# Softmax denominators: summed over key tiles on VectorE and GpSimd, one ones-matmul group per unit

## The reference

```
x = x + attn_a(layernorm(x));  x = x + ffn(layernorm(x))
x = x + attn_b(layernorm(x));  x = x + ffn(layernorm(x))
attn: qkv = h @ Wqkv + b; 16 heads of 32; scores = q k^T / sqrt(32), causal; softmax; @ v; @ Wo + bo
ffn:  (silu(h @ Wg^T) * (h @ Wu^T)) @ Wd^T, hidden 2048
```

## Time and profile before

| | |
|---|---|
| device time, median of 2 runs | 2245.22 us (2243.66 to 2246.78) |
| profiled execution | span 2243.9 us; its own device time is not recorded apart from the two above |
| TensorE busy | 2137.2 us (95%) |
| TensorE weight loads | 1502.9 us (67%) |
| VectorE busy | 1269.9 us (57%) |
| ScalarE busy | 531.7 us (24%) |
| GpSimd busy | 668.7 us (30%) |
| DMA | 135.10 MB in packets, mean 60 GB/s |
| granted TensorE clock | 0.982 in the mean |

### The profile page before, as it was taken

The page is one execution under the profiler, slowest core; times in us unless marked ns, Lnnn a source line. Parts: engine busy times, 40 slices in busy tenths (PEclk is TensorE's granted clock), DMA queues, the critical chain, the costliest instruction groups (busy, mean ns, idle before and its releaser), DMA issues.

```text
span 2243.9 us, 34194 instructions
## 1 busy us (share of the span) xinstructions
PE 2137.2 (95%) x11056; PEld 1502.9 (67%) x11056; DVE 1269.9 (57%) x2475; ACT 531.7 (24%) x1076; POOL 668.7 (30%) x508
## 2 busy tenths in 40 slices
PE   6999989999999999999989999999999999999998
PEld 5555478888755447888765554788886554578886
DVE  6767464545576646445447665544555666454444
ACT  1344410000144441000104454100011444310001
POOL 3323223332312322323231233232323223233332
PEclk9999999999999989999999999999999999999998
DMA  4332101111323211111142321111113232011112
GB/s 129 89 86 67 30 29 57 48 57 38 77 68 77 67 39 38 48 48 47 66 124 68 77 67 39 38 52 43 47 39 77 68 89 63 29 47 47 57 38 94
DMA packets 59745, 135.10 MB, mean 60 GB/s; under 512 B 10784, under 2 KB 11808, under 8 KB 59552
## 3 DMA queue, kind: packets, MB, share of 16 engines
q1 hardware_dynamic: 59552, 132.71, 20.9%
HBM read 77.62 MB, written 4.19 MB: 36 GB/s over the span
## 4 chain that ended last, share of the span: by engine, by line
PE 84%; issue 7%; DVE 4%; POOL 2%; ACT 1%; DMA 1%; SPq 1%; DVEq 0%; POOLq 0%; ACTq 0%
PE ring L872 13%; PE ring L873 13%; PE ring L874 13%; PE bank L982 12%; PE ring L936 8%; PE bank L960 7%; PE bank L872 6%; PE bank L873 6%; PE bank L874 6%; PE ring L863 1%; DVE attn L645 1%; POOL area L426 1%; DVE xn L682 1%; ACT prob L543 1%; DVE xn L645 1%
## 5 line engine op out<-in xcount | busy, mean ns | idle before, releaser
L872 PE MATMUL ring<-xt_hi,area 128*128 128x512 f32 x1248 | 492.0, 394 | 11.2 <-DVE xt_lo L654 8.1
L873 PE MATMUL ring<-xt_lo,area 128*128 128x512 f32 x1248 | 488.3, 391 | 0.0
L874 PE MATMUL ring<-xt_hi,area 128*128 128x512 f32 x1248 | 488.1, 391 | 0.0
L682 DVE CUSTOM_DVE_ANT_0 xn<-ring,mask_row 128x128 bf16<-128x128 f32 (+7 forms) x512 | 374.9, 750 | 131.4 <-PE ring L936 126.6
L543 ACT ACTIVATE prob<-bank 128x512 f32<-128x512 f32 (+3 forms) x768 | 335.4, 489 | 345.0 <-PE bank L960 344.0
L424 POOL TENSOR_SCALAR area<-w_stage 128x1024 fp32r<-128x1024 f32 x131 | 145.5, 1111 | 820.2 <-PE bank L874 432.5
L743 DVE TENSOR_TENSOR prob<-prob,ring 128x512 f32<-128x512 f32 x128 | 88.0, 687 | 450.2 <-ACT prob L561 450.1
L426 POOL TENSOR_TENSOR area<-w_stage,area 128x1024 fp32r<-128x1024 f32 x131 | 322.6, 2462 | 10.9
L561 ACT ACTIVATE prob<-ring 128x512 f32<-128x512 f32 x128 | 76.6, 598 | 999.5 <-PE ring L874 999.5
L872 PEld LDWEIGHTS ring<-xt_hi,area 128*128 128x128 f32 x1248 | 235.5, 189 | 71.3 <-issue 9.8
L874 PEld LDWEIGHTS ring<-xt_hi,area 128*128 128x128 f32 x1248 | 235.4, 189 | 49.8
(11 more groups left out here) (76 smaller groups left out, 2088.0 us busy)
## 6 DMA issues: line engine op xcount, KB each, us to landing
w_stage<-ffn_w SPq DMA_DIRECT2D x96, 512.0 KB, 3.3
area<-kq_parts SPq DMA_DIRECT2D x336, 128.0 KB, 2.3
w_stage<-attn_w SPq DMA_DIRECT2D x35, 512.0 KB, 3.3
x<-x_in SPq DMA_DIRECT2D x24, 256.0 KB, 3.7
area<-attn SPq DMA_DIRECT2D x48, 128.0 KB, 2.3
out<-x SPq DMA_DIRECT2D x16, 256.0 KB, 2.1
bias_rows<-row_bias SPq DMA_DIRECT2D x10, 256.0 KB, 4.1
area<-nm_hi SPq DMA_DIRECT2D x32, 8.0 KB, 1.8
```

The costliest lines, as they stand in the source:

```text
L682: dve.tensor_tensor_reduce(out=sum_out[:, RING[name] % 2, 0:keys], in0=src[:, 0:keys], in1=mask_row[:, TOKENS - keys:], scale=1.0, scalar= ...
L872: pe.matmul(dst, ah, bh, start=first and k == 0, stop=False)
L873: pe.matmul(dst, ah, bl, start=False, stop=False)
L874: ins = pe.matmul(dst, al, bh, start=False, stop=last and k == n - 1)
```

## The change

- TensorE no longer multiplies each step's `prob` with ones. VectorE (heads 0 and 1, `add_low`) and GpSimd (heads 2 and 3, `add_high`) add the `prob` tiles of a unit's key steps into `prob_sum` in SBUF, and one group of 4 ones-matmuls per unit (`denominators`) sums that over the partitions.
- `prob` gets a third buffer; the exponentials of a step wait for the values and for both sums of the step three back.
- `evacuate` copies out_bank only. ScalarE makes a first reciprocal as exp(-ln(den)) (`first_recip`), from one activation table set that is preloaded, and VectorE refines it with one Newton step folded into the normalisation: attn*r, then -den*r, then (that + 2)*attn*r.
- GpSimd's queue is written anew: masks, sums, weight split and attn splits interleaved by key step. VectorE's too. The attn of unit 6 is now split by VectorE, and the points of the last unit move by two half steps.

The core of it, with 12 columns of indentation taken off:

```diff
 def points(u):
...
-        return [9, 11, 13, 15, 23, 27]
+        return [11, 13, 15, 17, 25, 27]
...
-RECIPS = 8
+SPLIT_AFTER = (3, 1)
+ATTN_AFTER = {(5, 2): 0, (5, 3): 1, (5, 4): 2, (5, 5): 3, (6, 3): 4, (7, 2): 5}
+NORMALISE_AT = 3
+EXP_TABLE = "natural_log_exp_and_others"
...
-RECIPS_FROM = 6
-RECIPS_BETWEEN = 6
...
+PROB_BUFS = 3
+HALF = GH // 2
+ADD_BASE = [sum(key_tiles(v) - 1 for v in range(u)) for u in range(UNITS + 1)]
+ADDS = ADD_BASE[UNITS]
+POOL_SPLITS = UNITS - CHUNKS
+def added_through(u, j):
...
-        prob = sb("prob", [P, 2, GH, CHUNK])
+        prob = sb("prob", [P, PROB_BUFS, GH, CHUNK])
+        prob_sum = sb("prob_sum", [P, GH, CHUNK])
...
-    tile = prob[:, step % 2, :, d * P:(d + 1) * P]
+    tile = prob[:, step % PROB_BUFS, :, d * P:(d + 1) * P]
...
+def add_high(it, u, j):
+    step = J_BASE[u] + j
+    d = j - CT * unit(u)[1]
+    off = max(0, d) * P
+    heads = slice(HALF, GH)
+    wait_alone(pool, prob_ready, it * S2_STEPS + GH * (step + 1))
+    if d >= 0:
+        wait_alone(pool, mask_done, it * UNITS * CT + u * CT + d + 1)
+    new = prob[:, step % PROB_BUFS, heads, off:]
+    if j > 1:
+        wait_alone(pool, added_high, it * ADDS + ADD_BASE[u] + j - 1)
+        pool.tensor_tensor(prob_sum[:, heads, off:], prob_sum[:, heads, off:], new, ALU.add
+                           ).then_inc(added_high, 1)
+        return
+    old = prob[:, (step - 1) % PROB_BUFS, heads, :]
+    if u:
+        wait_alone(pool, sums_done, it * UNITS + u)
+    if off:
+        pool.tensor_copy(prob_sum[:, heads, :off], old[:, :, :off])
+    pool.tensor_tensor(prob_sum[:, heads, off:], old[:, :, off:], new, ALU.add).then_inc(added_high, 1)
 def split_attn(it, u):
...
-        if u in SPLIT_BEFORE:
-            split_weights(it, SPLIT_BEFORE[u])
-        for w in {5: range(5), 7: range(5, 7)}.get(u, ()):
-            split_attn(it, w)
-        for d in range(CT):
-            mask_probs(it, u, d)
-            if u == UNITS - 1 and d == 1:
+        for j in range(key_tiles(u)):
+            if j >= CT * unit(u)[1]:
+                mask_probs(it, u, j - CT * unit(u)[1])
+            if j:
+                add_high(it, u, j)
+            if j == SPLIT_AFTER[unit(u)[1]] and u in SPLIT_BEFORE:
+                split_weights(it, SPLIT_BEFORE[u])
+            if (u, j) in ATTN_AFTER:
+                split_attn(it, ATTN_AFTER[u, j])
+            if u == UNITS - 1 and j == CT + 1:
...
     def exps(u, j, heads):
...
-        if step >= 2:
-            act.wait_ge(pv_done, it * KEY_STEPS + step - 1)
+        if step >= PROB_BUFS:
+            added = it * ADDS + added_through(*step_of(step - PROB_BUFS))
+            act.wait_ge(pv_done, it * KEY_STEPS + step - PROB_BUFS + 1)
+            act.wait_ge(added_low, added)
+            act.wait_ge(added_high, added)
...
-            act.activation(prob[:, step % 2, h, off:], bank[n % 2][:, off:], ACT.Exp,
+            act.activation(prob[:, step % PROB_BUFS, h, off:], bank[n % 2][:, off:], ACT.Exp,
...
     def evacuate(u):
...
+        act.activation(attn[:, g, c * CHUNK:(c + 1) * CHUNK], out_bank[:, :], ACT.Copy
+                       ).then_inc(evacuated, 1)
+    def first_recip(u):
+        act.wait_ge(sums_done, it * UNITS + u + 1)
...
-        act.activation(recip[:, :], den_bank[:, :], ACT.Copy)
-        act.activation(attn[:, g, c * CHUNK:(c + 1) * CHUNK], out_bank[:, :], ACT.Copy
-                       ).then_inc(evacuated, 1)
+        act.activation(recip[:, :], den_bank[:, :], ACT.Ln).then_inc(log_done, 1)
+        act.wait_ge(log_done, it * UNITS + u + 1)
+        act.activation(recip[:, :], recip[:, :], ACT.Exp, scale=-1.0).then_inc(recip_done, 1)
     def silus(s, t):
...
+            if u and j == 1:
+                first_recip(u - 1)
...
+    evacuate(UNITS - 1)
+    first_recip(UNITS - 1)
...
-    evacuate(UNITS - 1)
...
-    load_table(ACT.Exp)
+    act.preload_act_table_set(EXP_TABLE)
...
-    def recip_part(u, n):
-        if n == 0:
-            dve.wait_ge(evacuated, it * UNITS + u + 1)
-        cols = slice(n * CHUNK // RECIPS, (n + 1) * CHUNK // RECIPS)
-        dve.reciprocal(recip[:, cols], recip[:, cols]).then_inc(recip_done, 1)
+    def add_low(u, j):
+        step = J_BASE[u] + j
+        d = j - CT * unit(u)[1]
+        off = max(0, d) * P
+        heads = slice(0, HALF)
+        dve.wait_ge(prob_ready, it * S2_STEPS + GH * step + HALF)
+        if d >= 0:
+            dve.wait_ge(mask_done, it * UNITS * CT + u * CT + d + 1)
+        new = prob[:, step % PROB_BUFS, heads, off:]
+        if j > 1:
+            dve.wait_ge(added_low, it * ADDS + ADD_BASE[u] + j - 1)
+            dve.tensor_tensor(prob_sum[:, heads, off:], prob_sum[:, heads, off:], new, ALU.add
+                              ).then_inc(added_low, 1)
+            return
+        old = prob[:, (step - 1) % PROB_BUFS, heads, :]
+        if u:
+            dve.wait_ge(sums_done, it * UNITS + u)
+        if off:
+            dve.tensor_copy(prob_sum[:, heads, :off], old[:, :, :off])
+        dve.tensor_tensor(prob_sum[:, heads, off:], old[:, :, off:], new, ALU.add).then_inc(added_low, 1)
     def normalise_attn(u):
...
-        dve.wait_ge(recip_done, (it * UNITS + u + 1) * RECIPS)
-        dve.tensor_tensor(attn[:, g, cols], attn[:, g, cols], recip[:, :], ALU.mult).then_inc(attn_ready, 1)
-    def split_last():
-        g, c = unit(UNITS - 1)
+        n = it * UNITS + u + 1
+        dve.wait_ge(recip_done, n)
+        dve.wait_ge(evacuated, n)
+        dve.tensor_tensor(attn[:, g, cols], attn[:, g, cols], recip[:, :], ALU.mult).then_inc(scaled, 1)
+        dve.wait_ge(scaled, n)
+        dve.scalar_tensor_tensor(recip[:, :], den_bank[:, :], -1.0, recip[:, :], ALU.mult, ALU.mult
+                                 ).then_inc(newton_done, 1)
+        dve.wait_ge(newton_done, n)
+        dve.scalar_tensor_tensor(attn[:, g, cols], recip[:, :], 2.0, attn[:, g, cols], ALU.add, ALU.mult
+                                 ).then_inc(attn_ready, 1)
+    def split_last(u):
+        g, c = unit(u)
...
-        dve.wait_ge(attn_ready, it * UNITS + UNITS)
+        dve.wait_ge(side_full, side_done(it, ("k", UNITS - 1)))
+        dve.wait_ge(attn_ready, it * UNITS + u + 1)
...
-        dve.wait_ge(last_hi_done, it + 1)
+        dve.wait_ge(last_hi_done, it * CHUNKS + c + 1)
...
-    for u in range(-1, UNITS - 1):
-        parts = list(range(RECIPS)) if u > 0 else []
-        def some_recips(count):
-            for n in parts[:count]:
-                recip_part(u - 1, n)
...
+            add_low(u - 1, key_tiles(u - 1) - 1)
+        if u < UNITS - 2 and u not in LO_BEFORE:
...
-            some_recips(RECIPS_BETWEEN)
...
-        for n, (what, *which) in enumerate(beside(u)):
+        for n, (what, *which) in enumerate(beside(u)[:early]):
...
-            if u < 0 and n in TAKE_AFTER:
-                take_v(CT + 2 + TAKE_AFTER.index(n))
-            if n == len(beside(u)) - 1:
-                some_recips(RECIPS)
-            elif n >= RECIPS_FROM:
-                some_recips(1)
-    for n in range(RECIPS):
-        recip_part(UNITS - 2, n)
-    normalise_attn(UNITS - 2)
-    for t in range(CT):
-        add_projected(t)
-    chunk_variance(it, 1, 0)
-    normalise_pair(it, 1, 0)
-    normalise_pair(it, 1, 1)
+        for j in range(1, key_tiles(u)):
+            if j > 1:
+                add_low(u, j - 1)
+            for (what, *which), at in zip(beside(u)[early:], points(u)):
+                if at // 4 + 1 == j:
+                    take[what](*which)
+            if u and j == NORMALISE_AT:
+                normalise_attn(u - 1)
+    u = UNITS - 1
+    add_low(u - 1, key_tiles(u - 1) - 1)
+    for j in range(2, key_tiles(u)):
+        add_low(u, j - 1)
+        if j == 2:
+            normalise_attn(u - 1)
+            split_last(u - 1)
+        for t in range(CT):
+            if points(u)[t] // 4 + 1 == j:
+                add_projected(t)
+        if j == CT + 1:
+            chunk_variance(it, 1, 0)
+        if j == CT + 2:
+            normalise_pair(it, 1, 0)
+            normalise_pair(it, 1, 1)
...
+    add_low(u, key_tiles(u) - 1)
...
-    for n in range(RECIPS):
-        recip_part(UNITS - 1, n)
-    normalise_attn(UNITS - 1)
-    split_last()
+    normalise_attn(u)
+    split_last(u)
...
-    def weigh(u, j, what):
+    def weigh(u, j):
...
-        if what == "values":
-            pe.wait_ge(prob_ready, it * S2_STEPS + GH * (step + 1))
-            if d >= 0:
-                pe.wait_ge(mask_done, it * UNITS * CT + u * CT + d + 1)
-            if j == 0 and not u:
-                pe.wait_ge(side_taken, side_done(it, ("k", 2)))
-            if j == 0 and u:
-                pe.wait_ge(evacuated, it * UNITS + u)
+        pe.wait_ge(prob_ready, it * S2_STEPS + GH * (step + 1))
+        if d >= 0:
+            pe.wait_ge(mask_done, it * UNITS * CT + u * CT + d + 1)
+        if j == 0 and not u:
+            pe.wait_ge(side_taken, side_done(it, ("k", 2)))
+        if j == 0 and u:
```

(35 more changed lines are left out.)

36 lines of the change are left out of this document (22 added, 14 removed).

## The result

| | before | after |
|---|---|---|
| device time, median of 2 runs | 2245.22 us | 2446.41 us (2446.30 to 2446.53) |
| ratio after / before | | 1.0893, interval 1.0867 to 1.0919 |
| profiled span | 2243.9 us | 2444.8 us |
| granted TensorE clock, mean | 0.982 | 0.918 |

The account below looks back on a forecast made before the run. TensorE was taken as the bound by totals, with VectorE taking over in long attention units. Per pass 7.9 + 1.0 - 2.0 - 0.5 - 3.5 = +2.9 us, four passes +12: 2257 us, range 2165 to 2315.

Parts of the forecast that it names:

- the sum for units 1, 3 and 5: Long attention units: VectorE at 29.9 us against TensorE's 21 becomes the bound; units 1, 3, 5 grow +7.9 us together.
- The sign that was set for it: Steps 2 to 7 of units 1, 3, 5: VectorE busy over 95%, units at 37 to 39 us, not 35.7.
- Units 6 and 7: Last two attention units of a pass: -0.5 us in unit 6; -3.5 in unit 7, which has almost no maxima.
- VectorE has the time there: Unit 7: first op tile gets its split from VectorE instead of GpSimd, priced at nothing.
- TensorE's term: Attention: 164.8 us of ones matmuls removed, 32 full groups added, net 131 us less, the whole possible gain.
- rival B: Whole kernel: TensorE is the bound throughout and VectorE's work hides; 2114 us, 2150 with half lost; chance 0.08.
- The lock: VectorE's sums and two normalisation operations wait for GpSimd at the shared SBUF port; 4.2 us per long unit.
- The clock: Attention: a thinner TensorE may be granted a lower clock; its cost is inside C's upper price.
- C: Units 1, 3, 5, steps 3 to 7: GpSimd late, VectorE second at the port; 2297 us, up to 2337; chance 0.26.
- A: Attention units: VectorE nearly always gets the port first; -12.8 us per pass, 2194 us; chance 0.22.
- D: ScalarE, each unit: Ln and Exp in different table sets cost table loads, up to +82, 2327 us; chance 0.02.
- The third buffer's new waits: Exponentials: three prob buffers remove one wait and add two, for both sums of three steps back; priced at nothing.

Follow-up runs that it names:

- the moved sums: The changed kernel with VectorE's sum of each step put behind the step's maxima instead of ahead of them: 2479.02 us, ratio 1.1044.

## Why the prediction was wrong, point by point

The account that the runs give, from before to after: the ones matmuls -35; Ln, Exp and Newton +11; the new order and third buffer +48; the sums +178 (72 for VectorE's, 93 for GpSimd's, 13 for both being there). From 2245 that is 2447. Each entry is a difference of two runs, on chips whose times for the kernel before differ by about 4 us, and is known to some 5 to 8 us. That the sums and the new order cost this is shown by leaving them out. By which waits they do it is read from the traces.

The miss of 189 us is 47 per pass. The windows of the first pass put it here: 19 in units 1, 3 and 5 (priced +7.9, measured +27.1), 22 in units 6 and 7 (priced -4.0, measured +18.1), and 5.5 in units 2 and 4 (priced -2.0, measured +3.5); the rest is in unit 0.

- **The step that failed** is in the sum for units 1, 3 and 5: "VectorE becomes the bound and the unit grows by 2.6". The unit's length was taken as the larger of two engines' work, 29.9 us against 21, as if everything else ran in the shadow of the larger. VectorE's added work was right to about 1 us in unit 1 (+8.9 measured over the whole unit, +7.8 priced from step 1 on) and short in units 3 and 5 (+9.5 measured against 7.8, +11.7 against 7.3; the windows of the same cut before have 25.47 and 27.15 us of VectorE). But unit 1 grew by 9.0, unit 3 by 7.3 and unit 5 by 10.8. VectorE, busy 25.5 of 35.8 us in unit 1 before, had 10.4 us idle; after, it was busy 34.3 of 44.8 and had 10.5. In units 3 and 5 its idle time went from 10.3 to 8.1 and from 8.9 to 8.0. So it did not become the bound in the sense of the sum. The sign that was set for it, VectorE busy over 95% in steps 2 to 7, did not come either: from 105 us to the end of unit 1 it is busy 27.6 of 32.2 us, 86%. That the unit grew by just VectorE's added work is partly chance, since the runs divide the 9.0 otherwise: -2.7 for the ones matmuls, +0.1 for the reciprocals, +4.1 for the new order, +3.6 for VectorE's sums, +2.6 for GpSimd's, +1.3 for both together.
- **Units 6 and 7**, priced at -0.5 and -3.5, came out at +7.6 and +10.5, and this is as large a part of the miss. With few maxima unit 7 was thought free of VectorE, and for VectorE's sums that was right. With the sums cut it is at +1.9, with VectorE's sums cut at +8.1, with GpSimd's cut at +1.9: there it is GpSimd's sums that cost it. The term had only VectorE's and TensorE's work in it, none of GpSimd's. "VectorE has the time there", of the split of unit 6's attn that the change gives it, put at nothing what became the wait of 5.2 us: VectorE's two operations for it took 2.38 and 2.71 us beside GpSimd's work. Of unit 6's +7.6, +3.7 stays with the sums cut and is the new order's.
- **TensorE's term.** "Net 131 us less ... the whole possible gain" was never all in the sum, which took 6.0 us a pass of it, in units 2, 4, 6 and 7. The removal alone gave 35 us, 8.8 a pass: 0.9, 0.9 and 0.8 in units 2, 4 and 6, close to the price, 1.7 in unit 7, half of it, and 2.7, 2.0 and 1.7 in units 1, 3 and 5, where nothing was counted. So this term is not where the forecast went wrong; but rival B, at 2114 to 2150, lay below what even the removal alone reached (2210).
- **The lock.** The kind was right, and the Trainium skill's rule (SBUF — State Buffer, § Who interferes with whom) with it: by that rule a second operand in PSUM frees VectorE, and the trace agrees, 1214 ns against 2214. The size was low by half for the wide sums: 0.5 us per operation priced, 1.0 measured, and 0.8 and 0.5 for L790 and L795. The row gave 0.7 when scaled by GpSimd's share, and the prediction took less, a value between that and a VectorE that is always first. A scaling by share alone also assumes that the two meet at random, while both wait for the same exponentials; that this makes up the rest is likely and not tested. GpSimd pays as well: its first sum of a unit, L496, took 3444 ns, and 2401 with VectorE's sums cut.
- **The clock.** The fall was priced only "inside C's upper price". At two levels, a mean of 0.918 over 2445 us is an estimate of 2 x 0.082 x 2445 = 400 us at the lower one, against 80 before. Matmuls that run at half speed through 320 us more make up about 160 us of TensorE's busy time, and that is what is found: 2172 measured against 2137 - 131 = 2006. How much of it is lost time for the kernel the runs do not separate.
- **The rivals.** A and B are refuted (L772's mean is 2214, not 1.22 us; no unit shrank). D is refuted: 9 table loads, as before. C named the right place, GpSimd coming out of a weight split with two sums owed, and the right order of events. Its sign held: weight loads of value groups waited 27 us for masks where the line was drawn at 10. Its price of 80 was less than half of the 189 that the kernel took over the forecast. It counted the waits on the port in units 1, 3 and 5, not the stops of TensorE behind them, and nothing in units 6 and 7.
- **The third buffer's new waits**, priced at nothing: right for the order as built (ScalarE waited 16.1 us for GpSimd's first sums and 5.1 for VectorE's), and fragile, as the moved sums showed (89.3).
- **What held:** L936's kind of waits over 103.6 (148.8), the unchanged FFN stretch, undisturbed sums at 1.22 (L780), GpSimd's at about 2.5, VectorE's added work in unit 1.

What stays open: by which waits GpSimd's sums cost 6 us in units 3 and 5; how much the clock costs; which part of the new order costs 4 us in unit 1 and the 2 us in unit 7 that the wait for the split leaves (the placing of the attn splits and ones groups was tried, and only moved the loss); and the third buffer, which was never tried apart from the new order. No variant that computes the whole softmax beat the kernel before; the best that the old order would allow with free sums is 2210 to 2221.

## What to carry to other kernels

When a stage hands tiles round three engines through two-buffer rings, do not price a change as the larger of the engines' sums. First ask how much shorter the stage gets if the removed work is simply left out (here 35 of 131 us). For the added work, an engine's idle time is not room that it can fill: in the long units with maxima 6 us of added work on VectorE cost 3.6 to 5.5, and 13 us on GpSimd cost 3 to 6, though neither engine was full. Here the add that TensorE does by accumulating in PSUM was cheap (leaving 160 of 192 groups out won 35 us) and the same add on VectorE and GpSimd was dear (178 us). Price each engine that gets work, and each operation that changes its engine, however small. Follow a long wait back through every in-order queue it stands behind: the 6.7 us here were made of a weight split, two owed sums, a normalisation and a sum.

## What was not expected of the hardware

- A VectorE add of two SBUF operands waits for GpSimd even when it moves two elements: 648 ns in the mean beside GpSimd's sums against 213 without them, the longest 2344, with medians of 165 and 159. With one operand in PSUM the 1024-element add took 1214 ns beside the same GpSimd work.
- 165 us of added matmuls in the changed kernel raised the mean granted clock from 0.918 to 0.952 and cost 23 us. After TensorE had stood for 6.24 us, in the stretch from 120 to 140 the granted clock was 0.73, between the levels of 1.2 and 2.4 GHz.
- Ln and Exp of 512 columns took 601 and 631 ns on ScalarE, like a copy (598), from one table set.
